# Window attention and a graph layer: outputs divided two slots at a time, tasks ahead of the outputs in odd slots, norm statistics combined on GpSimd

## The reference

```python
def _mhsa(x, w_qkv, b_qkv, w_o, b_o, mask):
    qkv = x @ w_qkv + b_qkv
    ...
    scores = einsum('bqhd,bkhd->bhqk', q, k) / sqrt(16)
    if mask is not None:
        scores = scores + mask[:, None, :, :]
    attn = softmax(scores, axis=-1)
    out = einsum('bhqk,bkhd->bqhd', attn, v).reshape(B, S, D)
    return out @ w_o + b_o
...
x = x + _L0_conv_ref(_ln_c(x), ...)       # eps 1e-6
t = t + _L0_ffn_ref(_ln_t(t), ...)        # eps 1e-5
```

## Time and profile before

| | us |
|---|---|
| median of 3 runs | 8065.56 |
| lowest and highest run | 8052.8 and 8068.06 |
| profiled execution, its own time | 8049.89 |
| profiled execution, span from first to last instruction | 8047.8 |
| mean granted TensorE clock of that execution | 0.683 |
| busy: TensorE, weight loads | 4220.0, 2317.6 |
| busy: VectorE, ScalarE, GpSimd | 5078.9, 2132.1, 4933.0 |

### The profile page before, as it was taken

The page is one execution under the profiler, slowest core; times in us unless marked ns, Lnnn a source line. Parts: engine busy times, 40 slices in busy tenths (PEclk is TensorE's granted clock), DMA queues, the critical chain, the costliest instruction groups (busy, mean ns, idle before and its releaser), DMA issues. The chain is left out here.

```text
span 8047.8 us, 104795 instructions
## 1 busy us (share of the span) xinstructions
PE 4220.0 (52%) x31501; PEld 2317.6 (29%) x31501; DVE 5078.9 (63%) x15628; ACT 2132.1 (26%) x3826; POOL 4933.0 (61%) x5216
## 2 busy tenths in 40 slices
PE   5889999898434534534534434435435445445200
PEld 3666666665211211211211212212212212112000
DVE  9999999999545545445445445455455455455378
ACT  4667777776100100100100100100101101001034
POOL 2232222221677777777777777777777777777673
PEclk8999999999655655655655655655655656656555
DMA  1122212221211111111111111111111111111267
GB/s 49 50 56 57 58 53 57 57 59 47 54 33 44 32 32 44 32 32 44 32 32 44 32 32 44 32 38 38 32 42 34 32 44 32 32 44 32 79 211 251
DMA packets 503710, 419.08 MB, mean 52 GB/s; under 512 B 160530, under 2 KB 400194, under 8 KB 502722
## 3 DMA queue, kind: packets, MB, share of 16 engines
q1 hardware_dynamic: 289138, 323.26, 12.3%
q0 software_dynamic: 147552, 56.96, 7.2%
q10 hardware_dynamic: 66560, 33.56, 1.4%
HBM read 203.37 MB, written 176.45 MB: 47 GB/s over the span
## 5 line engine op out<-in xcount | busy, mean ns | idle before, releaser
L1569 POOL DMA_INDIRECT edge_G<-node_rows,edge_src x4352 | 4160.6, 956 | 1326.1 <-issue 1326.1
L1618 PE MATMUL edge_cbank<-edge_ohh,edge_ohl 128*128 128x256 bf16 x4096 | 1416.0, 395 | 2944.8 <-DVE edge_ohh L1386 2856.2
L1618 PEld LDWEIGHTS edge_cbank<-edge_ohh,edge_ohl 128*128 128x128 bf16 x4096 | 427.6, 104 | 3926.6 <-DVE edge_ohh L1386 3754.9
L1386 DVE TENSOR_SCALAR edge_ohh<-edge_iob,edge_dlf 128x256 bf16<-128x256 bf16 x4096 | 1194.2, 298 | 0.0
L1385 DVE TENSOR_SCALAR edge_ohl<-edge_iob,edge_dlf 128x128 bf16<-128x128 bf16 x4096 | 1084.3, 266 | 14.8 <-DVE edge_dlf L1379 14.5
L1594 ACT ACTIVATE edge_hid<-edge_hbank,edge_b1c 128x512 f32<-128x512 f32 x512 | 351.7, 687 | 2496.9 <-PE edge_hbank L1625 2496.9
L556 POOL TENSOR_SCALAR attn_nw<-attn_mv 128x8 f32<-128x8 f32 x64 | 86.5, 1351 | 1499.8 <-DVE attn_mv L982 1499.7
L1344 DVE COPY edge_O<-edge_O 128x24 f32<-128x24 f32 x64 | 12.6, 197 | 1530.3 <-DMA edge_G<-node_rows,edge_src 1530.3
L1398 DVE TENSOR_TENSOR edge_yo<-edge_ybank,edge_b2r 128x512 f32<-128x512 f32 x256 | 177.0, 691 | 948.5 <-PE edge_ybank L1634 948.5
L1597 ACT ACTIVATE edge_w<-edge_w 128x272 f32<-128x272 f32 x64 | 27.5, 429 | 2407.5 <-DVE edge_w L1358 2407.5
L1625 PE MATMUL edge_hbank<-edge_xt,edge_w 128*128 128x512 f32 x1024 | 591.7, 728 | 1.3 <-ACT edge_hid L1594 1.3
(11 more groups left out here) (239 smaller groups left out, 6496.4 us busy)
## 6 DMA issues: line engine op xcount, KB each, us to landing
edge_G<-node_rows,edge_src POOLq DMA_INDIRECT x4352, 2.4
expert_out<-edge_yo SPq DMA_DIRECT2D x64, 1024.0 KB
comb_ye<-expert_out SPq DMA_DIRECT2D x32, 2048.0 KB, 11.9
state_rows<-edge_O SPq DMA_DIRECT2D x64, 816.0 KB, 3.5
attn_km<-attn_kT SPq DMA_DIRECT2D x1024, 32.0 KB, 2.0
attn_xin<-in_x SPq DMA_DIRECT2D x32, 512.0 KB, 4.2
attn_xres<-in_x SPq DMA_DIRECT2D x32, 512.0 KB, 5.1
x_rows<-attn_x SPq DMA_DIRECT2D x32, 512.0 KB, 3.1
```

The source lines that it names most:

```text
L1386: dve.tensor_scalar(ohh[:, t % RING, :], iob[:, :], dlf[:, 1, t:t + 1], None, ALU.is_equal).then_inc(s_oh, 1)
L1569: pool.indirect_dma_start(G[b][:, t, :], None, node_rows, bass.IndirectOffsetOnAxis(ap=src[b][:, t:t + 1], axis=0)).then_inc(s_g[b][2 * t ...
L1618: pe.matmul(cbank[b][:, 0:HI], ohl[:, t % RING, :], ohh[:, t % RING, :], start=(t == 0), stop=(t == HC - 1)).then_inc(s_ohp, 1)
```

## The change

1. *Division.* The two output banks become one tensor of two banks, and VectorE divides two pairs at a time, in odd slots: one reciprocal and one product over both banks. `s_nrm` and `s_recip` count pairs of slots.
2. *Order on TensorE.* The weighing of an even pair, which stands in an odd slot, now waits for the division of the two pairs before it, and follows the slot's tasks. The weighing of an odd pair (even slots) stays ahead of the tasks and waits for no division.
3. *Statistics.* The aggregation on VectorE goes, with its two waits. GpSimd makes mean and variance from the six numbers itself: its chain has fifteen instructions instead of nine.

```diff
--- before.py
+++ after.py
@@ -246,6 +246,7 @@
 HWIN = WGRID * WGRID // 2
 KM_DONE = 16 * HEADS
 SETUP = 8
+OUT_SLOTS = 2
 NEG = -1.0e9
 SCALE = HDIM ** -0.5
 EPS_LN = 1e-6
@@ -306,15 +307,14 @@
         mx = sb("mx", [P, PAIRS, 2, 2, HEADS // 2])
         pT = [sb(f"pT{i}", [P, 2, GROUPS, P]) for i in range(2)]
         att = [sb(f"att{h}", [P, PAIRS // 2, 2, P]) for h in range(2)]
-        rsum = [sb(f"rsum{i}", [P, 2, HEADS]) for i in range(2)]
+        rsum = [sb(f"rsum{i}", [P, OUT_SLOTS, 2 * HEADS]) for i in range(2)]
         attT = [sb(f"attT{s}", [P, BANK]) for s in range(2)]
         st6 = [sb(f"st6{i}", [P, TILES, 6]) for i in range(2)]
-        mv = [sb(f"mv{i}", [P, TILES, 2]) for i in range(2)]
-        nw = [sb(f"nw{i}", [P, 5, TILES]) for i in range(2)]
+        nw = [sb(f"nw{i}", [P, 8, TILES]) for i in range(2)]
 
         score_bank = ps("score", [P, 2, BANK])
         turn_bank = ps("turn", [P, 2, BANK])
-        out_bank = [ps("out0"), ps("out1")]
+        out_bank = ps("out", [P, OUT_SLOTS, BANK])
         misc = [ps("misc0"), ps("misc1")]
 
         s_w = sem("s_w")
@@ -549,13 +549,20 @@
 
             def deviation(k, m):
 
-                v, half, y, h, shift = (nw[k][:, i, :] for i in range(5))
+                v, half, y, h, shift, gap, square, total = (nw[k][:, i, :] for i in range(8))
                 eps = (EPS_LN, EPS_TOKEN)[k]
-
-                pool.wait_ge(s_moment[k], (2, 4)[k] * (m + 1))
-                pool.tensor_scalar(v, mv[k][:, :, 1], eps, None, ALU.add)
-                pool.tensor_scalar(half, mv[k][:, :, 1], eps, -0.5, ALU.add, ALU.mult)
-                link(pool.tensor_scalar(shift, mv[k][:, :, 0], -1.0, None, ALU.mult))
+                (mean0, sum0), (mean1, sum1) = ((st6[k][:, :, 3 * i + 1], st6[k][:, :, 3 * i + 2]) for i in range(2))
+
+                pool.wait_ge(s_moment[k], (1, 2)[k] * (m + 1))
+                pool.tensor_tensor(shift, mean0, mean1, ALU.add)
+                pool.tensor_tensor(total, sum0, sum1, ALU.add)
+                link(pool.tensor_tensor(gap, mean0, mean1, ALU.subtract))
+                pool.tensor_scalar(total, total, 1.0 / P, eps, ALU.mult, ALU.add)
+                link(pool.tensor_tensor(square, gap, gap, ALU.mult))
+                link(pool.tensor_scalar(square, square, 0.25, None, ALU.mult))
+                link(pool.tensor_tensor(v, total, square, ALU.add))
+                pool.tensor_scalar(half, v, -0.5, None, ALU.mult)
+                link(pool.tensor_scalar(shift, shift, -0.5, None, ALU.mult))
                 link(pool.tensor_tensor(y, v, minus_half[:, :], ALU.pow))
                 link(pool.tensor_tensor(h, y, y, ALU.mult))
                 link(pool.tensor_tensor(h, h, half, ALU.mult))
@@ -779,7 +786,7 @@
                 st, h = STREAM[task[0]], int(task[2])
                 t = take(n, task)
                 k = n - LAG[task] + LAG[task[0]]
-                pe.wait_ge(s_nrm, k * PAIRS + 4 * h + 4)
+                pe.wait_ge(s_nrm, (k * PAIRS + 4 * h + 4) // OUT_SLOTS)
                 for i in range(PAIRS // 2):
                     last = pe.transpose(t[:, i * P:(i + 1) * P], att[h][:, i, st, :], ident[:, :])
                 return last
@@ -873,8 +880,9 @@
                 last.then_inc(s_pt, 1)
 
             def weigh(n, j):
-                if n * PAIRS + j >= 2:
-                    pe.wait_ge(s_nrm, n * PAIRS + j - 1)
+                if j % OUT_SLOTS == 0 and n * PAIRS + j > 0:
+
+                    pe.wait_ge(s_nrm, (n * PAIRS + j) // OUT_SLOTS)
                 pe.wait_ge(s_pte, n * PAIRS + j + 1)
                 for s in streams(n):
                     st, m = STREAM[s], n - LAG[s]
@@ -883,7 +891,7 @@
                     for g in range(GROUPS):
                         for e in range(2):
                             c = st * GROUPS * VW + g * VW
-                            last = pe.matmul(out_bank[j % 2][e * WTOK:(e + 1) * WTOK, c:c + VW],
+                            last = pe.matmul(out_bank[e * WTOK:(e + 1) * WTOK, j % OUT_SLOTS, c:c + VW],
                                              pT[j % 2][:, st, g, e * WTOK:(e + 1) * WTOK], vx[st][:, 2 * j + e, g, :],
                                              start=True, stop=True)
                 last.then_inc(s_pv, 1)
@@ -903,11 +911,14 @@
                     if streams(k):
                         turn(k, i)
                     k, i = later(n, j, 3)
-                    if streams(k):
+                    if streams(k) and i % OUT_SLOTS:
                         weigh(k, i)
                     for task in tasks_of(n, j):
                         kind = turned if task[0] == "S" else KINDS[task[:2]]
                         kind(n, task).then_inc(s_full[where(n, task)[0]], 1)
+                    if streams(k) and i % OUT_SLOTS == 0:
+
+                        weigh(k, i)
 
         @block.vector
         def _(dve):
@@ -964,23 +975,13 @@
                 dve.wait_ge(s_loops, 1)
                 dve.tensor_scalar(rows, rows, NODE_BITS, None, ALU.logical_shift_left).then_inc(s_loops, 1)
 
-            moments = [0, 0]
-
-            def moment(k, ins):
-                ins.then_inc(s_moment[k], 1)
-                moments[k] += 1
-                dve.wait_ge(s_moment[k], moments[k])
-
             def statistics(k, src, tiles, m):
                 if m > 0:
 
                     dve.wait_ge(s_stat[k], m)
                 for j in tiles:
                     last = dve.bn_stats(st6[k][:, j, :], src[:, j, :])
-                moment(k, last)
-                for j in tiles:
-                    last = dve.bn_aggr(mv[k][:, j, :], st6[k][:, j, :])
-                moment(k, last)
+                last.then_inc(s_moment[k], 1)
 
             def sorting():
 
@@ -1070,19 +1071,21 @@
                 dve.sem_inc(s_x2, 1)
 
             def normalised_output(n, j):
-                dve.wait_ge(s_pv, n * PAIRS + j + 1)
+
+                dve.wait_ge(s_pv, n * PAIRS + j + OUT_SLOTS)
                 lo, hi = span(n)
-                o = out_bank[j % 2][:, 0:2 * GROUPS * VW].rearrange("p (s h d) -> p s h d", s=2, d=HDIM + 1)[:, lo:hi]
-                r = rsum[j % 2][:, lo:hi, :]
+                k = (n * PAIRS + j) // OUT_SLOTS
+                o = out_bank[:, :, lo * GROUPS * VW:hi * GROUPS * VW].rearrange("p j (h d) -> p j h d", d=HDIM + 1)
+                r = rsum[k % 2][:, :, lo * HEADS:hi * HEADS]
                 if j % 4 == 0:
                     for s in streams(n):
                         if n - LAG[s] > 0:
 
                             wait_full(dve, f"{s}o{j // 4}", n - LAG[s] - 1)
                 dve.reciprocal(r, o[:, :, :, HDIM]).then_inc(s_recip, 1)
-                dve.wait_ge(s_recip, n * PAIRS + j + 1)
-                dve.tensor_tensor(att[j // 4][:, j % 4, lo:hi, :].rearrange("p s (h d) -> p s h d", h=HEADS),
-                                  o[:, :, :, 0:HDIM], r.unsqueeze(3).to_broadcast([P, hi - lo, HEADS, HDIM]),
+                dve.wait_ge(s_recip, k + 1)
+                dst = att[j // 4][:, j % 4:j % 4 + OUT_SLOTS, lo:hi, :].rearrange("p j s (h d) -> p j (s h) d", h=HEADS)
+                dve.tensor_tensor(dst, o[:, :, :, 0:HDIM], r.unsqueeze(3).to_broadcast([P, OUT_SLOTS, (hi - lo) * HEADS, HDIM]),
                                   ALU.mult).then_inc(s_nrm, 1)
 
             def less_maximum(n, j):
@@ -1101,8 +1104,8 @@
             for n in steps:
                 for j in range(PAIRS):
                     k, i = later(n, j, 4)
-                    if streams(k):
-                        normalised_output(k, i)
+                    if streams(k) and i % OUT_SLOTS == OUT_SLOTS - 1:
+                        normalised_output(k, i + 1 - OUT_SLOTS)
                     if streams(n):
                         less_maximum(n, j)
                     if j == 4 and 0 <= n + 2 < IMAGES:
```

## The result

The changed kernel takes 8175.04 us (median of 4 runs, 8168.94 to 8177.77) where the kernel before takes 8063.6 us: ratio 1.0136, interval 1.0123 to 1.0148. It is slower, as forecast, but by 111 us instead of 46 and 25 us above the top of the range.

A forecast was written before the change was run, and what follows sets the result against it. VectorE was taken to pace the first stage's middle, with TensorE within 1.4 us a step. Middle +46, early -8, 600 to 700 us +6, drain -2 and GpSimd +4 give +46 us: 8110 us, range 8000 to 8150.

The forecast's parts named there:

- What bounds, and what is next: Middle of the first stage: VectorE paces the step, TensorE waits for it only 1.4 us a step and paces afterwards.
- The sum: Whole kernel: middle +46 us, early -8, 600 to 700 us +6, drain -2, GpSimd +4; together +46 us.
- The early steps: Steps from 100 to 600 us, where TensorE waits 5.3 us a step for VectorE: -8 us over nine steps.
- VectorE's terms: VectorE in a step: aggregation 1.5 us less and division in pairs 1.0 us less, together 2.5 us (1.5 to 3.9).
- GpSimd: Statistics chain with six more instructions: costs only at the end of the first stage, +4 us (0 to 8), once.
- The moved weighing: TensorE in slots 1, 3, 5, 7: weighing goes from filling a stall to behind it, +3.7 us a step (2.5 to 4.2).
- The clock: TensorE's granted clock, 0.99 in the middle: its work stays the same, so no term was given.
- VectorE pacing on (1): Rival: the moved weighing is covered and all VectorE saves is gained, 79 us less 4: 7990 us; chance 0.25.
- the even outcome (2): Rival: weighing costs about 2 us, middle loses 12 us, early steps gain as much: 8050 to 8082 us; chance 0.12.
- The wait for the division (3): Rival: odd-slot weighing also waits for VectorE's division, 20 to 40 us beyond the forecast: 8130 to 8150 us; chance 0.08.
- Pairs as dear as two (4): Rival: a pair's division costs as much as two, VectorE saves 1.5 us a step only: 8114 us; no separate chance.

## Why the prediction was half right

*What bounds, and what is next.* Right. VectorE and TensorE were within 1.4 us of each other; VectorE got some 2 us less, TensorE more, and TensorE paces the middle. A middle step took 59.5 us and not the 58.5 that I had from counting transposes: the edges of the window cut in a group more than 1200 us hold. The sum does not hang on it. The early steps did not gain 8 us but lost 1 to 9 (557.6 us, 565.3 in the repetition, 556.7 before); what took the 8 us and more there was not looked into.

*VectorE's terms.* Right: 57.6 to 55.4 us busy in a step, for a forecast of 2.5 less. The pair takes 0.35 and 0.69 us, and from reciprocal to next reduction 0.99. The aggregation of eight saved 0.79 us between the statistics and the next sort instruction, a little over the 0.67 counted.

*GpSimd.* Right in kind, high in size. At the end of the stage ScalarE's wait for the chain went from 10.47 us to 11.52, as the timeline shows:

```profile
2148.76 3.18 ACT L688 ACTIVATE attn_normed<-attn_x,attn_nw 128x128 f32<-128x128 f32 x8 [11.52 <-POOL attn_nw L571]
```

One us, not four: the chain itself grew by 2.1 us, from 8.0 to 10.1, and the aggregation ahead of it went. For VectorE I had taken no cost of GpSimd's longer chain. With GpSimd's statistics alone VectorE's busy time in a middle step fell from 57.4 to 55.9 us, the 1.5 that the aggregation took, and the kernel gained 40 us, so no such cost shows.

*The moved weighing.* Right in mechanism and sum, in part by luck in the slots. The third task of slot 1 waits 2.02 us for a forecast of 1.8; the two key waits grew by 21.6 and 23.9 us in the window for a forecast of some 20 each. Slot 3, for which I took 0.6 us of a possible 1.05, lost 1.1 us a step (6.8 us in 20.2 steps, 27.5 in 18.6), and slot 7, for which I took 1.0, lost 0.4 (21.4 and 27.6 us): two errors that cancel. The four together grew by 4.1 us a step for my 3.7, TensorE's whole idle time by 2.6 for my 2.3. Steps at nearly full clock are 2.4 us longer than before, by the line 61.0 against 59.4, 1.6 us. Over 20 steps that is 32 to 52 us for my 46. The run with the order alone shows that it carries all of the loss. The two in which the weighing fills the wait again, or the evacuation comes early, take the loss back, which shows that the place behind the evacuation is why.

*The clock: the step that failed.* "its work stays the same, so the clock gets no term". The work stayed the same, and the clock fell from 0.99 to 0.94. That is 2.4 us a step by busy time and 3.0 by the line, 48 to 60 us in 20 steps, as much as the term that I did size or more; with it the sum would have been 94 to 106, around the 100 us that the stage lost. In the traces the clock fell when waits were added, to 0.94 and with the order alone to 0.93, and came back when several of them went: in the changed kernel to 0.97 with the late normalisations, with and without the weighing behind the second task, and to 0.98 with both and slot 7's transposes moved. Why it falls with waits was not shown. I had read 0.99 as a property of the work alone, and not also of where its waits stand. How much of the two terms would be there without the other was not tried apart: no run changes the clock alone.

*The rivals.* VectorE pacing on (1) and the even outcome (2) fell with the waits for scores. The wait for the division (3) did not appear in the changed kernel, only in the one with the order undone, which shows that the order does hide it. Pairs as dear as two (4) fell by the rows.

**What stays open** is which idle time brings the clock down. Partly filling the waits of three slots left it at 0.94; emptying slot 7 of slow stretches left more of them in slot 5; mending slot 5 alone, or all but it, took back part. Of the window's 1200 us, 22 to 35 are at the lower clock in the kernels with the old order and one division a slot, 44 to 117 where part of the waits is mended or the order undone, 137 to 169 in the changed kernel, with the order alone, with the filled waits and with slot 7 emptied; no run ties the loss to one wait. Nor is it the amount of idle time in a step. With late normalisations in the changed kernel TensorE is idle 5.4 us of a step, with the weighing behind the second task as well 5.0, both less than the 5.9 of the kernel before; yet 80 and 68 us are at the lower clock there, and 27 before.

## What to carry to other kernels

Work that fills a wait is not free to move: put behind the wait it adds up to its whole length (1.05 us a slot here), so place it between the tasks on either side of the wait, or bring forward the evacuation that ends it; either turned +1.4% into -0.1 or -0.2%. And where a change adds or moves idle time of a TensorE that just keeps its full clock (0.99 here, 0.94 after the change), give the clock a term of its own, sized from rows of the same work at either level (16 score matmuls: 1.09 us at 1.00, 1.98 at 0.50).

## What the runs showed of the hardware

- The same TensorE matmuls were granted 0.94 instead of 0.99 of the full clock when waits in four slots of a step grew to as much as 1.5 to 2.0 us, in 26 stretches of 5.8 us on average at a clock of 0.50, within 1200 us: 16 score matmuls took 1.98 us for 1.09. Longer matmuls cost 2.4 us a step, idle time 2.6.
- The clock did not follow the amount of idle time: 5.4 us of it in a step went with 80 us of 1200 at the lower clock in one kernel, 5.9 us with 27 in another.
- Putting two other tasks ahead of a stall emptied slot 7 of slow stretches and left as much time at the lower clock (154 us of 1200, 150 before that edit), with 20 of 26 stretches in slot 5 (11 of 29 before it). Bringing an evacuation forward in slots 1 and 5 removed theirs (13 of 26) and cut the whole from 150 to 80 us of 1200.
- Taking eight aggregations and two semaphore waits from VectorE saved 0.79 us between the statistics and the next sort instruction, while six more instructions on GpSimd made a dependent chain 2.1 us longer, 10.1 for 8.0.
